# A convolution, scan and mixture kernel on one core: first-layer blocks moved ahead, six gelu buffers, and four moves in the order of the other engines

## Time and profile before

| | |
|---|---|
| median of three runs | 383.43 us (382.65 to 384.72) |
| the profiled execution | 381.92 us, span 380.1 us |
| busy in the span | PE 324.4 (85%), DVE 316.3 (83%), ACT 276.4 (73%), POOL 268.1 (71%) |
| prologue, loop, tail | first scan at 57.3; gates of bodies 1 to 7 at 93.2 to 317.7; gate of the tail at 352.0 |

### The profile page before, as it was taken

How to read it: one execution, slowest core, us unless ns; L and a number is a source line. 1 busy time by engine, 2 the same in 40 slices (tenths; PEclk the granted TensorE clock), 3 DMA queues, 4 the chain that set the end, 5 groups by cost and what they waited for, 6 DMA issues and landing times. The chain is left out here.

```text
span 380.1 us, 5564 instructions
## 1 busy us (share of the span) xinstructions
PE 324.4 (85%) x1689; PEld 181.3 (48%) x1689; DVE 316.3 (83%) x424; ACT 276.4 (73%) x465; POOL 268.1 (71%) x268
## 2 busy tenths in 40 slices
PE   0596899596999979988998899889988997899795
PEld 0476455341745355535552555345534553463563
DVE  2774457997699989998999899989999998999533
ACT  1002458678887998799889987998797886874483
POOL 8903505785678988897889779977998797877110
PEclk9997999559699999999999999999998999899999
DMA  8944039989989989985997599759976995000000
GB/s 179 251 88 85 2 98 228 225 176 216 219 213 224 223 200 219 232 192 124 220 227 174 138 218 220 167 133 227 225 156 166 230 212 126 3 0 3 14 0 16
DMA packets 21301, 59.54 MB, mean 157 GB/s; under 512 B 4988, under 2 KB 13336, under 8 KB 15384
## 3 DMA queue, kind: packets, MB, share of 16 engines
q1 hardware_dynamic: 20104, 58.35, 67.7%
q10 hardware_dynamic: 1168, 0.84, 0.9%
HBM read 53.94 MB, written 5.24 MB: 156 GB/s over the span
## 5 line engine op out<-in xcount | busy, mean ns | idle before, releaser
L354 POOL TENSOR_TENSOR hs<-hs,Cs 128x1024 f32<-128x1024 f32 x63 | 149.4, 2377 | 22.1 <-DVE hs L834 21.4
L834 DVE TENSOR_TENSOR_SCAN hs<-av,P 128x1024 f32<-128x1024 f32 x64 | 146.3, 2286 | 2.7 <-POOL av L347 0.6
L828 DVE TENSOR_TENSOR P<-P,ub 128x1024 f32<-128x1024 f32 x62 | 76.0, 1225 | 2.8 <-DMA ub<-u_scratch 1.6
L674 ACT ACTIVATE hb<-P,b1c 128x512 f32<-128x512 f32 x112 | 70.9, 686 | 10.0 <-PE P L1303 9.0
L1317 PE MATMUL P<-hb,W2s 128*64 128x256 f32 x448 | 60.3, 391 | 0.0
L1302 PE MATMUL P<-X,W1H 128*128 128x512 f32 x112 | 50.6, 451 | 3.0 <-ACT hb L674 2.6
L615 ACT ACTIVATE av<-P,Aneg 128x510 f32<-128x510 f32 x68 | 43.9, 677 | 7.7 <-PE P L1239 4.2
L1303 PE MATMUL P<-X,W1L 128*128 128x512 f32 x112 | 44.9, 401 | 0.0
L1317 PEld LDWEIGHTS P<-hb,W2s 128*64 128x64 f32 x448 | 27.3, 136 | 27.9 <-issue 19.5
L1239 PE MATMUL P<-D,selD 128*128 128x512 f32 x64 | 30.8, 524 | 11.3 <-ACT av L615 10.5
L615 ACT ACTIVATE av<-av,Aneg 128x510 f32<-128x510 f32 x60 | 38.3, 708 | 1.1 <-DMA av<-dt_scratch 1.0
(11 more groups left out here) (230 smaller groups left out, 557.1 us busy)
## 6 DMA issues: line engine op xcount, KB each, us to landing
ub<-u_scratch SPq DMA_DIRECT2D x31, 1024.0 KB, 11.1
av<-dt_scratch SPq DMA_DIRECT2D x15, 1024.0 KB, 7.4
dt_scratch<-dts SPq DMA_DIRECT2D x7, 256.0 KB, 2.9
u_scratch<-rl SPq DMA_DIRECT2D x7, 256.0 KB, 2.9
av<-in_L_conv_Wr SPq DMA_DIRECT2D x2, 576.0 KB, 7.0
av<-in_L_conv_Wl SPq DMA_DIRECT2D x2, 576.0 KB, 8.6
res<-in_x SPq DMA_DIRECT2D x4, 256.0 KB, 4.9
hb<-in_L_ffn_W SPq DMA_DIRECT2D x2, 512.0 KB, 6.0
```

The source lines that it names most:

```text
L354: gp.tensor_tensor(hs[:, at, :, :], hs[:, at, :, :], rep(Cs[:, p, :], 1, 2), ALU.mult).then_inc(S["cm"], 1)
L674: a_.activation(hb[:, r % 4, :], P[:, (XA, XB)[r % 2], :], ACT.Gelu, bias=b1c[:, r:r + 1]).then_inc(S["gl"], 1)
L828: v.tensor_tensor(ring, rep(P[:, BB, :], 1, 2), ub[:, 2 * n:2 * n + 2, :], ALU.mult).then_inc(S["bm"], 1)
L834: v.tensor_tensor_scan(hs[:, (SLOTS * g + n) % RING].rearrange("p a t -> p (a t)"), av[:, 2 * n:2 * n + 2, :].rearrange("p a t -> p (a t)" ...
```

## The change

- `hb` has six buffers instead of four, and `rt` six rows instead of twelve (its rows are renumbered, not shown).
- TensorE: f1(0) goes to bank XB and f1(1) to bank XD, then XA and XB in turn. f1(0) stands where two `pe_warm` matmuls stood, ahead of `pe_c`; f1(1), f1(2), f1(3) follow it. The pairs give way to a written order, in which five second-layer blocks, f2(11) to f2(15), come behind the next projection. The evictions and the weight spreads move one gelu pair later on ScalarE.
- The banks XC and XD change places in the second layer, and the weight transposes and the bias go to XC.
- VectorE: `dve_slot` is cut into `dve_product` and `dve_scan`; slot 2's product is issued between `dve_router1` and `dve_router2`.
- GpSimd: `pool_slot` 7 comes ahead of weighted(4).
- Tail: VectorE makes the full normed product first and one half of X2, GpSimd copies the other half; one of the last two output stores is issued by ScalarE.

```diff
+        HB = 6
+        hb = sb("hb", [128, HB, T])
+        F1_BANK = (XB, XD) + (XA, XB) * (KC * EXP // 2 - 1)
...
             sp_out(sp_, G - 2, 0)
-            sp_out(sp_, G - 1, 1)
+            sp_out(sp_, G - 1, 1, (0,))
...
-                weighted(4)
                 if nxt is not None:
                     pool_slot(eng, i, p, 7)
+                weighted(4)
...
+            eng.wait_ge(S["xn2"], 2 * G)
+            eng.wait_ge(S["f1"], LAST)
+            gp.tensor_copy(X2[0:64, 0:HW], xn[0:64, :]).then_inc(S["xh2"], 1)
             pool_router(eng, G - 1)
...
-                since(eng, "f2", EXP * KC * g + max(r - 3, 0))
-                a_.activation(hb[:, r % 4, :], P[:, (XA, XB)[r % 2], :], ACT.Gelu, bias=b1c[:, r:r + 1]).then_inc(S["gl"], 1)
+                since(eng, "f2", EXP * KC * g + max(r + 1 - HB, 0))
+                a_.activation(hb[:, r % HB, :], P[:, F1_BANK[r], :], ACT.Gelu, bias=b1c[:, r:r + 1]).then_inc(S["gl"], 1)
...
-                        if n == 3 and nxt is not None:
+                        if n == 4 and nxt is not None:
                             act_dhi(eng, nxt)
                         if n == 1:
+                            act_wt(eng, prev)
+                        if n == 2:
                             if nxt is not None:
                                 act_c(eng, nxt, q, YS)
-                            act_wt(eng, prev)
-                        if n == 2:
                             act_bias(eng, prev)
-                        if n in range(2, 6):
-                            act_wb(eng, prev, n - 2)
+                        if n in range(3, 7):
+                            act_wb(eng, prev, n - 3)
...
+            sp_out(eng, G - 1, 1, (1,))
...
                     dve_router1(eng, prev)
+                dve_product(eng, i, 2)
+                if prev is not None:
                     dve_router2(eng, prev, nxt2)
-                dve_slot(eng, i, 2)
+                dve_scan(eng, i, 2)
...
-            for h in range(2):
-                q = slice(64 * h, 64 * h + 64)
-                v.tensor_tensor(X2[q, HW * h:HW * h + HW], P[q, XB, 0:HW], rqs[q, :], ALU.mult).then_inc(S["xh2"], 1)
             v.tensor_tensor(xn, P[:, XB, 0:HW], rqs[:, :], ALU.mult).then_inc(S["xn2"], 2)
+            v.tensor_tensor(X2[64:128, HW:T], P[64:128, XB, 0:HW], rqs[64:128, :], ALU.mult).then_inc(S["xh2"], 1)
             eng.wait_ge(S["xn2"], 2 * G)
-            eng.wait_ge(S["xh2"], 2 * G)
-            for h in range(2):
+            for h in (1, 0):
                 q, o = slice(64 * h, 64 * h + 64), slice(64 - 64 * h, 128 - 64 * h)
+                eng.wait_ge(S["xh2"], 2 * G)
                 low = v.tensor_tensor(X2[o, HW * h:HW * h + HW], xn[q, :], X2[q, HW * h:HW * h + HW], ALU.subtract)
...
             if r == 0:
                 eng.wait_ge(S["xl2"], g + 1)
+            if r == 1:
+                eng.wait_ge(S["xn1"], so_far(g, 4))
+                since(eng, "me", EXP * g)
+            if r == 2:
                 eng.wait_ge(S["sp_relu"], so_far(g, 2))
                 eng.wait_ge(S["aexp"], NBLK * so_far(g, 2))
-            if r >= 2:
+            if r == 3:
+                eng.wait_ge(S["gl"], EXP * KC * g + 1)
+            if r >= 4:
                 eng.wait_ge(S["gl"], EXP * KC * g + r - 1)
...
                 if prev is not None:
-                    eng.wait_ge(S["xn2"], 2 * (prev + 1))
-                    pe_warm(eng, 2, XB)
+                    pe_f1(eng, prev, 0)
                 if nxt is not None:
                     pe_c(eng, nxt)
                 if prev is not None:
-                    pe_pair(eng, prev, 0)
+                    pe_f1(eng, prev, 1)
                     pe_f1(eng, prev, 2)
                     pe_f1(eng, prev, 3)
                     pe_f2(eng, prev, 0)
                     pe_f2(eng, prev, 1)
                     pe_wt(eng, prev)
-                    for n in range(2, 6):
-                        pe_pair(eng, prev, n)
-                        if n == 2:
+                    for n, (fill, back) in enumerate(((4, (2, 3)), (6, (4, 5)), (8, (6,)), (10, (7, 8)), (12, (9,)), (14, (10,)))):
+                        pe_f1(eng, prev, fill)
+                        pe_f1(eng, prev, fill + 1)
+                        for r in back:
+                            pe_f2(eng, prev, r)
+                        if n == 0:
                             pe_bias(eng, prev)
-                        pe_wb(eng, prev, n - 2)
-                    for n in range(6, 8):
-                        pe_pair(eng, prev, n)
+                        elif n < 5:
+                            pe_wb(eng, prev, n - 1)
                 if nxt2 is not None:
                     pe_proj(eng, nxt2)
                 if prev is not None:
-                    pe_pair(eng, prev, 8)
+                    for r in range(11, 16):
+                        pe_f2(eng, prev, r)
```

More of the change, by code:

```diff
@@ L169, in build @@
         X2 = sb("X2", [128, T], f32r)
-        rt = sb("rt", [128, 12, 4, EXP])
+        rt = sb("rt", [128, 6, 4, EXP])
         rv = sb("rv", [128, 8, 4])
@@ L272, in sp_spread, with sp_out @@
                 sp_.dma_start(ub[:, 4 * c:4 * c + 4, :], rep(u_dram[p][:, 4 * c:4 * c + 4, :], 0, ST)).then_inc(S[f"u_in{c}"], 16)
-        def sp_out(sp_, g, p):
+        def sp_out(sp_, g, p, halves=(0, 1)):
             sp_.wait_ge(S["acc"], EXP * (g + 1))
-            for h in range(2):
+            for h in halves:
                 sp_.dma_start(ov[h, :, g:g + 1, :], acc[64 * h:64 * h + 64, 0:1, :]).then_inc(S["out_sem"], 16)
@@ L399, in pool_router @@
             eng.wait_ge(S["o2"], g + 1)
-            gp.tensor_tensor(rt[:, 9], rt[:, 8], rep(rv[:, 2], 2, EXP), ALU.mult).then_inc(S["num"], 1)
+            gp.tensor_tensor(rt[:, 3], rt[:, 2], rep(rv[:, 2], 2, EXP), ALU.mult).then_inc(S["num"], 1)
             eng.wait_ge(S["num"], g + 1)
-            gp.tensor_tensor(rt[:, 10], rt[:, 9], rt[:, 4], ALU.add).then_inc(S["wt"], 1)
+            gp.tensor_tensor(rt[:, 4], rt[:, 3], rt[:, 1], ALU.add).then_inc(S["wt"], 1)
             eng.wait_ge(S["wt"], g + 1)
             eng.wait_ge(S["rden"], g + 1)
-            gp.tensor_tensor(rt[:, 11], rt[:, 10], rep(rv[:, 5], 2, EXP), ALU.mult).then_inc(S["wn"], 1)
+            gp.tensor_tensor(rt[:, 5], rt[:, 4], rep(rv[:, 5], 2, EXP), ALU.mult).then_inc(S["wn"], 1)
             eng.wait_ge(S["wn"], g + 1)
-            w4 = rt[:, 11].rearrange("p (q h) e -> p q h e", h=2)
+            w4 = rt[:, 5].rearrange("p (q h) e -> p q h e", h=2)
             since(eng, "wtr", 2 * g)
@@ L649, in act_router @@
             eng.wait_ge(S["dd"], g + 1)
-            a_.activation(chances, rt[:, 1], ACT.Exp).then_inc(S["ex"], 1)
+            a_.activation(chances, rt[:, 0], ACT.Exp).then_inc(S["ex"], 1)
         def act_wt(eng, g):
@@ L655, in act_wt @@
             eng.wait_ge(S["k_wt"], 1)
-            a_.activation(wT[0:32, :], P[0:32, XD, 0:HW], ACT.Copy).then_inc(S["wtc"], 1)
+            a_.activation(wT[0:32, :], P[0:32, XC, 0:HW], ACT.Copy).then_inc(S["wtc"], 1)
         def act_bias(eng, g):
@@ L660, in act_bias @@
             since(eng, "acc", EXP * (g - 1) + 2)
[L661 removed]
+            a_.activation(t1[:, 1, :], P[:, XC, HW:T], ACT.Copy).then_inc(S["bt"], 1)
         def act_wb(eng, g, r):
@@ L815, in dve_slot, with dve_product @@
         def dve_slot(eng, g, n):
+            dve_product(eng, g, n)
+            dve_scan(eng, g, n)
+        def dve_product(eng, g, n):
             c = n // 2
@@ L828, in dve_slot, with dve_scan @@
                 v.tensor_tensor(ring, rep(P[:, BB, :], 1, 2), ub[:, 2 * n:2 * n + 2, :], ALU.mult).then_inc(S["bm"], 1)
+        def dve_scan(eng, g, n):
+            c = n // 2
             eng.wait_ge(S["bm"], SLOTS * g + n + 1)
@@ L890, in dve_router2 @@
             eng.wait_ge(S["ms1"], g + 1)
-            v.tensor_tensor(rt[:, 4], ranked, bc(1), ALU.is_equal).then_inc(S["o1"], 1)
+            v.tensor_tensor(rt[:, 1], ranked, bc(1), ALU.is_equal).then_inc(S["o1"], 1)
             eng.wait_ge(S["o1"], g + 1)
-            v.scalar_tensor_tensor(out=left, in0=rt[:, 4], scalar=-2.0, in1=chances, op0=ALU.mult, op1=ALU.add).then_inc(S["e2"], 1)
+            v.scalar_tensor_tensor(out=left, in0=rt[:, 1], scalar=-2.0, in1=chances, op0=ALU.mult, op1=ALU.add).then_inc(S["e2"], 1)
             eng.wait_ge(S["e2"], g + 1)
@@ L926, in dve_last @@
             at = HW * (e // 2 % 2)
-            v.scalar_tensor_tensor(out=mes[:, e % 4, :], in0=P[:, (XC, XD)[e % 2], at:at + HW],
+            v.scalar_tensor_tensor(out=mes[:, e % 4, :], in0=P[:, (XD, XC)[e % 2], at:at + HW],
                                    scalar=cols[:, R["b2"] + e:R["b2"] + e + 1], in1=wbs[:, e, :],
@@ L1268, in pe_wt @@
             eng.wait_ge(S["vlo"], g + 1)
-            eng.wait_ge(S["xn1"], so_far(g, 4))
-            since(eng, "me", EXP * g)
             for q in range(2):
```

(20 more changed lines are left out.)

21 lines of the change are left out of this document (5 added, 16 removed).

## The result

| | before | after |
|---|---|---|
| median | 383.04 us | 390.26 us (386.99 to 391.98, 4 runs) |
| ratio after to before | | 1.019, 95% interval 1.0151 to 1.0228 |
| profiled execution, span | 381.92, 380.1 | 391.41, 389.7 |

The forecast was 379.5, in a range of 374.5 to 384.5. The result lies outside, with the other sign: it is the third rival, the falling clock, and dearer than priced there.

The account below looks back on a forecast made before the run. VectorE paces the old kernel at 37.13 us; afterwards TensorE's chain through f2(11) bounds it. Gains 1.70 (iterations 1 to 5) + 0.70 + 0.50 (6 and 7) + 0.43 + 0.55 (tail) = 3.9: 379.5 us, range 374.5 to 384.5.

Parts of the forecast that it names:

- the third rival: TensorE's clock falls at f1(0) to f1(3), losing 1.4 us per iteration after a gap of about 0.6: 386.5 us, chance 0.12.
- GpSimd's last slot: Slot 7 ahead of an addition: starts 0.65 us sooner, the gate loses its 0.35 wait, the split of X2 comes 0.5 later.
- at nothing: f1's wait for the split costs 0: f1(0) begins some 9 us after the gate, the first gelu needs it at 11.21.
- The product: Slot 2's product ahead of the marks fills VectorE's router wait; scan 1.26 us earlier, all spent waiting at line 916.
- The loop: Gate to gate in iterations 1 to 5: 11.21 + 17.50 + 8.08 = 36.79 us, a gain of 0.34 each, 1.70 together.
- that term: TensorE's projection starts 0.16 us after ScalarE's last gelu, bounds 0.05 and 0.39.
- VectorE as pacemaker: VectorE, busy 35.02 of the 37.13 us period, keeps the pace if f2(11) and the sums come early enough; chance 0.08.
- The first rival: f2(11) comes by 27.44 and VectorE sets a period of 35.52 us: time about 372.9, chance 0.08.
- The tail: After the loop: one half-product step fewer saves 0.43 us, the second output store issued by ScalarE saves 0.55.

## Why the prediction was wrong, point by point

**The step that failed** is the one on GpSimd's last slot: "In exchange GpSimd idles 0.5 and is 0.5 later with step input and with the split of X2", and "That f1 waits for the split I count at nothing". The split came 1.12 later after the gate than before (9.55 against 8.43), and 1.35 later than with slot 7 behind the addition (8.20), since the addition that would lie in GpSimd's waiting time now lies behind it. The 0.5 rested on slot 7's scan ending at 202.85, as if the third message did not wait; but two steps further on the forecast itself makes that message wait 1.2, and slot 7's scan stands behind it. With it GpSimd waits 1.85, and slot 7 had not been late at all. And the count "at nothing" asked only when the first gelu needs f1, not what TensorE does until then: it stood 1.29, and then ran at half its clock for 3.5 to 7.0 us.

**The clock's rival** named the place, the cause and the sign, and was given 0.12. Two sizes were off: the gap (0.6 for 1.29) and the price (1.4 per iteration; against the 37.06 with five idle products the four periods lost 39.22 - 37.06 = 2.16 on average), so that it said 386.5 for 390.26. The 1.4 was worked out for a low stretch of the length seen in the earlier trace rows; where the stretch had about that length, 3.5 us, the loss was 38.66 - 37.06 = 1.60, and where it was twice as long, which the rival did not foresee, 39.76 - 37.06 = 2.70. The argument against it, a clock of 1.00 in the earlier trace rows, was read from a kernel that kept TensorE at work there. The Trainium skill's TensorE: Matmul & The Clock Gate, Part 1, has the slow clock as the default that activity lifts; the 0.55 behind the pause of 1.29 agrees.

**The product** did what was said: no router wait, and its gain spent at the third message, 1.20 to 1.27 for the 1.27 forecast. **The loop** with slot 7 behind the addition is 36.88 for 36.79: from the gate to the first gelu 10.97 (181.06 - 170.09) for 11.21, from there to the third message 17.79 for 17.50, and 8.12 for 8.08 to the gate. The sum is right in part by luck: 0.24 too much and 0.29 too little nearly cancel. The projection started 0.39 after the last gelu in the kernel with two idle products, the upper bound of that term.

**VectorE as pacemaker** was half of it. The kernel without the first-layer order took the router's waits from VectorE and gained nothing per iteration: the circle of ScalarE and TensorE was as long. The Trainium skill's Perfetto Trace Analysis, Identifying the Most-Contended Engine, would have that engine improved first; the trace agrees only once the circle is shorter too. The first rival's way was then open, but by one more step: with block 11 ahead the period is 35.95, where it said 35.52 with slot 7 first (35.83 to 35.88 measured).

**The tail** gave 0.32 up to the end of the subtractions (362.16 to 369.36 is 7.20, against 7.52 before) and 0.31 behind the last addition (2.68 against 2.99): 0.63 for the 0.98 forecast. GpSimd's copy ends at 368.40, with VectorE's half product (368.41), so it is not late:

```profile
367.52 0.43 DVE L1136 TENSOR_TENSOR xn<-P,rqs 128x256 f32<-128x256 f32 x1
367.98 0.43 DVE L1137 TENSOR_TENSOR X<-P,rqs 64x256 fp32r<-64x256 f32 x1
368.51 0.85 DVE L1142 TENSOR_TENSOR X<-xn,X 64x256 fp32r<-64x256 f32 x2
```

```profile
368.01 0.39 POOL L546 CAST X<-xn 64x256 fp32r<-64x256 f32 x1 [4.29 <-DVE xn L1136]
```

Two stores from two engines took 0.47 and 0.54 beside each other for 1.11 one behind the other, but only 0.31 of that reached the end.

**Open**: why the low stretch, and the period with it, alternates between two lengths from body to body, and why a pause of 0.92 costs the clock in one body and not in the next.

## What to carry to other kernels

Work of an engine that waits anyway is free where it stands and costs its full length behind the wait: before moving an addition, see whether it lies in idle time, in the kernel as the other steps will leave it. A wait that a forecast finds (here of 1.2 at the third message) is to be carried into every other step and then attacked itself: with slot 7 back in its place, one block put into the 0.6 in front of the projection took the gain from 0.5% to 1.7%. Where TensorE is to wait in front of dense work, read the granted clock behind such waits in other stages of the same trace, and price a fall by how long the clock then stays low, which here was 3.5 us in some iterations and twice that in others.

## What the runs showed of the hardware

In body 4 of the kernel after, a pause of TensorE of 1.29 us, behind a stretch in which it was busy 1.74 of 3.20, was followed by 3.4 us at a granted clock of 0.55; the same pause came in each of bodies 2 to 5, and the low stretch was 3.5 us long in bodies 2 and 4 and 6.9 to 7.0 us in bodies 3 and 5. In the profiled runs pauses of 0.84 to 0.86 (two idle products ahead of them) kept 1.00 in bodies 2 to 5, and pauses of 0.92 (none) went either way. Slot 7's place on GpSimd, an engine busy 69% of the span, was worth 390.26 - 380.63 = 9.6 us in the kernel after (two groups of runs, in which the kernel before stood at 383.04 and 382.34).
